# A scan in three stages, spread over the half phases of an eight-part hybrid kernel

## Time and profile before

| | |
|---|---|
| median of the runs | 1622.7 us |
| the profiled execution | 1631.55 us |
| its span, first to last instruction | 1629.8 us |
| mean granted TensorE clock, share of full speed | 0.755 |
| PE, DVE, ACT, POOL busy | 1043.3, 912.9, 745.1, 629.3 us |
| instructions | 18052 |

### The profile page before, as it was taken

The page is one execution under the profiler, slowest core; times in us unless marked ns, Lnnn a source line. Parts: engine busy times, 40 slices in busy tenths (PEclk is TensorE's granted clock), DMA queues, the critical chain, the costliest instruction groups (busy, mean ns, idle before and its releaser), DMA issues.

```text
span 1629.8 us, 18052 instructions
## 1 busy us (share of the span) xinstructions
PE 1043.3 (64%) x5080; PEld 769.7 (47%) x5080; DVE 912.9 (56%) x2789; ACT 745.1 (46%) x2034; POOL 629.3 (39%) x672
## 2 busy tenths in 40 slices
PE   4777788377877554885877624467667536673282
PEld 2454577246664234573755212456456215461172
DVE  4676565485758754656566728164565644646011
ACT  4786676366557544454655413244353232441020
POOL 2102100552414365404232564734443565355503
PEclk8656699587877567787888656788888757886596
DMA  8001243402220122243422211233433222331362
GB/s 246 1 1 66 68 150 110 126 20 104 91 78 12 52 70 78 84 143 100 135 98 65 64 39 43 91 135 102 142 136 110 72 61 87 127 104 47 126 224 90
DMA packets 101812, 150.65 MB, mean 92 GB/s; under 512 B 9840, under 2 KB 72688, under 8 KB 101584
## 3 DMA queue, kind: packets, MB, share of 16 engines
q1 hardware_dynamic: 88832, 129.20, 24.2%
q0 software_dynamic: 8528, 18.19, 3.7%
q10 hardware_dynamic: 4352, 2.10, 0.4%
HBM read 125.39 MB, written 28.25 MB: 94 GB/s over the span
## 4 chain that ended last, share of the span: by engine, by line
PE 33%; DVE 27%; ACT 12%; issue 12%; POOL 9%; DMA 5%; another core or an unknown queue 2%; SPq 1%; POOLq 0%; DVEq 0%; ACTq 0%
DVE Pw L882 9%; PE eo_bank L1290 9%; PE h_bank L1275 8%; ACT sc_bank L635 6%; DVE rings L892 5%; PE sc_bank L1224 5%; POOL xg L562 3%; POOL gbuf L575 2%; DVE nmx L829 2%; PE sc_bank L1168 2%; PE mix_bank L1147 2%; DMA gbuf<-yg,pos 2%; DVE eos L1014 2%; DVE qk L816 2%
## 5 line engine op out<-in xcount | busy, mean ns | idle before, releaser
L1290 PE MATMUL eo_bank<-wring,hid 128*128 128x128 f32 x1472 | 230.5, 307 | 96.9 <-DVE eos L1014 89.3
L882 DVE SCALAR_TENSOR_TENSOR Pw<-rings,bc,du 128x128 f32<-128x128 f32 x512 | 252.3, 553 | 64.8 <-ACT rings L680 64.8
L1275 PE MATMUL h_bank<-xT,wring 128*128 128x128 f32 x1472 | 238.4, 313 | 60.3 <-DVE xT L1002 49.7
L1290 PEld LDWEIGHTS eo_bank<-wring,hid 128*128 128x128 f32 x1472 | 210.9, 220 | 109.4 <-issue 85.2
L1275 PEld LDWEIGHTS h_bank<-xT,wring 128*128 128x128 f32 x1472 | 214.3, 221 | 97.6 <-DVE xT L1002 63.7
L635 ACT ACTIVATE sc_bank<-sc_bank,nmx 128x256 f32<-128x256 f32 x512 | 229.7, 456 | 53.0 <-DVE nmx L829 45.9
L508 POOL TENSOR_TENSOR rings<-Rs,Abc 128x512 f32<-128x512 f32 x128 | 161.9, 1280 | 208.6 <-ACT Rs L663 114.7
L709 ACT ACTIVATE hid<-h_bank 128x512 f32<-128x512 f32 x184 | 109.4, 595 | 286.3 <-PE h_bank L1275 256.2
L1224 PE MATMUL sc_bank<-Pw,upto 128*128 128x512 f32 x256 | 171.2, 769 | 81.0 <-DVE Pw L882 81.0
L829 DVE TENSOR_REDUCE nmx<-sc_bank 128x2 f32<-128x512 f32 x256 | 170.2, 685 | 71.8 <-PE sc_bank L1168 48.8
L575 POOL DMA_INDIRECT gbuf<-yg,pos x128 | 122.6, 957 | 177.9 <-issue 104.1
(11 more groups left out here) (155 smaller groups left out, 1359.2 us busy)
## 6 DMA issues: line engine op xcount, KB each, us to landing
wring<-wcat SPq DMA_DIRECT2D x184, 512.0 KB
stage<-xg SPq DMA_DIRECT2D x40, 256.0 KB
yg<-eos SPq DMA_DIRECT2D x40, 256.0 KB
wcat<-in_w SPq DMA_DIRECT2D x16, 256.0 KB, 5.6
X<-in_x SPq DMA_DIRECT2D x16, 128.0 KB, 5.5
xg<-xnb,pos POOLq DMA_INDIRECT x128
gbuf<-yg,pos POOLq DMA_INDIRECT x128
out<-X ACTq DMA_DIRECT2D x16, 128.0 KB
```

Of the source, the lines that this page charges most:

```text
L882: last = dve.scalar_tensor_tensor(out=Pw[:, c, n * D:(n + 1) * D], in0=e, scalar=bc[:, c, n:n + 1], in1=du[:, c, :], op0=ALU.mult, op1=ALU ...
L1275: last = pe.matmul(hb[b % 2][:, f], wring[:, n % WR, 0, f], xT[:, b % 2], start=True, stop=True)
L1290: last = pe.matmul(eo[:, o:o + P], hid[:, b % 2, f], wring[:, n % WR, 1, f], start=(k == 0), stop=(k == FC - 1))
```

## The change

The scan gets a third stage. A sequence has its front in phase 9 + b, its chunks (`middle`) a phase later and its tail two phases later, so three sequences are in the scan at once; attention goes on in each of phases 0 to 15. There are 33 phases instead of 37. Chunk k's E, L and r stand at half 2k, P at 2k + 1, S at 2k + 2 and X at 2k + 3 of the middle phase (S and X of chunk 7 in the tail's first halves); POOL's phase is now a loop over halves, with exponents at even halves, the first two at halves 13 and 15 of the front's phase.

The chunk sums have one bank of their own, and scores two instead of three. bc, du, Rs, y, uD and xnb are doubled, rec slots are 8. Attention's v moves from the mix bank to the prep bank; the scan's output and the second layer's preparation move from the prep bank to the mix bank, with statistics tiles of their own. A group's 16 scatters go one at each half of a phase, the gathers of the next phase's front one at each of halves 10 to 13, the final gathers at halves 5 to 8. Routing of the second layer moves to the phase after the group's last tail.

Per phase the new schedule has: blocks 9, 10, 4 in phases 6 to 8; 10, 10, 3 in 10 to 12; 10, 10, 3 in 14 to 16; 15, 13, 14, 4 in 17 to 20; 12, 11 in 21 and 22; 13, 10 in 25 and 26; 15, 8 in 29 and 30. Scatters are in phases 5, 9, 13, 16, 17, 20, 24 and 28.

```diff
-    NSC = 3
+    NSC = 2
...
-    FILL = 2 * GS
+    SCAN_FIRST = 2 * GS + 1
...
-        bc = sb("bc", [P, T, 2 * N])
+        bc_b = sb("bc_b", [P, 2, T, 2 * N])
...
         delta = sb("delta", [P, T, P])
-        du = sb("du", [P, T, P])
-        Rs = sb("Rs", [P, T, P])
-
-
-        SLOTS, REC_SLOTS = 4, 6
+        du_b = sb("du_b", [P, 2, T, P])
+        Rs_b = sb("Rs_b", [P, 2, T, P])
+
+
+        SLOTS, REC_SLOTS = 4, 8
         rings = sb("rings", [P, SLOTS + REC_SLOTS, 4 * D])
         Pw = sb("Pw", [P, T, N * D])
         ysum = sb("ysum", [P, 4 * D])
-        y_s = sb("y_s", [P, T, P])
...
-            xnb[ly] = sb(f"xnb{ly}", [P, GT, P])
+            xnb[ly] = sb(f"xnb{ly}", [P, 2, GT, P])
...
+        ss = bank("sum_bank")
...
+        prep_bank = {1: mp, 2: ma}
...
-        AT_LATE = 3
+        GATHER_HALVES = range(10, 14)
+        FINAL_HALVES = range(5, 9)
...
+        scan_dve = Parts(Progress(sem("scan_dve"), ["st0", "stats0", "stats1", "u0", "u", "dpre", "dneg", "delta", "du"]),
+                         Progress(sem("scan_in_dve"), [f"P{k}" for k in chunks]),
+                         Progress(sem("scan_out_dve"), [f"X{k}" for k in chunks]),
+                         Progress(sem("scan_add_dve"), ["x3"]))
...
-        RUN_FIRST = {(1, 0): (6, 1, 40), (1, 1): (10, 1, 60), (1, 2): (17, 1, 46), (2, 0): (20, 1, 46), (1, 3): (25, 1, 30),
-                     (2, 1): (27, 1, 30), (2, 2): (30, 1, 30), (2, 3): (34, 0, 25)}
...
+        RUN_FIRST = {(1, 0): (6, 0, 40), (1, 1): (10, 0, 38), (1, 2): (14, 0, 38), (2, 0): (17, 0, 26), (1, 3): (18, 10, 28),
+                     (2, 1): (21, 0, 32), (2, 2): (25, 0, 30), (2, 3): (29, 0, 25)}
...
-            head[b if b < FILL else FILL + 2 * (b - FILL)] = b
-            tail_a[b + 1 if b < FILL else FILL + 1 + 2 * (b - FILL)] = b
-            f = FILL + 1 + 2 * b if b < FILL else 3 * FILL + (b - FILL)
-            front[f] = b
-            tail_s[f + 1] = b
-        for g, n in enumerate(([23, 24, 25, 26], [29, 30, 31, 31], [32, 33, 33, 33], [36, 36, 36, 36])):
-            for q in range(GS):
-                final.setdefault(n[q], []).append(GS * g + q)
-        PHASES = 37
+            head[b], tail_a[b + 1] = b, b
+            n = SCAN_FIRST + b
+            front[n], middle[n + 1], tail_s[n + 2] = b, b, b
+        final = {n: list(range(b, e)) for n, b, e in ((20, 0, 1), (21, 1, 2), (22, 2, 3), (23, 3, 4), (24, 4, 5), (25, 5, 6), (26, 6, 7), (27, 7, 8),
+                                                      (28, 8, 10), (29, 10, 12), (31, 12, 14), (32, 14, 16))}
+        PHASES = 33
...
-            return [(ly, b // GS) for ly, at in ((1, tail_a), (2, tail_s)) for b in [at.get(n - 1)] if b is not None and b % GS == GS - 1]
...
+            return [(1, tail_a[n - 1] // GS)] if tail_a.get(n - 1, 0) % GS == GS - 1 else \
+                [(2, tail_s[n - 2] // GS)] if tail_s.get(n - 2, 0) % GS == GS - 1 else []
...
+            def scatter_rows(ly, g, n):
 
                 r = RUNS.index((ly, g))
-                pool.wait_ge(*route_dve[ly].at("pos", g))
-                if r:
-                    for j in range(STORES):
-                        pool.wait_ge(s_xg[j], 16 * r)
-                else:
-                    pool.wait_ge(s_zero, 16)
-                for n in range(NSLOT):
-                    pool.indirect_dma_start(xg, bass.IndirectOffsetOnAxis(ap=pos[ly][:, g % 2, n:n + 1], axis=0),
...
+                for half in range(HALVES):
+                    if half == 0 and a is not None:
+                        attn_residual(a)
+                    if half == 0 and ct is not None:
+                        scan_sum(ct, 6)
+                    if half == 2 and ct is not None:
+                        scan_sum(ct, 7)
+                    if half == 3 and ct is not None:
+                        scan_skip(ct)
+                    if half == 3 and c is not None:
+                        scan_rest(c)
+                    if cm is not None and half in range(2, 14, 2):
+                        scan_exponents(cm, half // 2 + 1)
+                    if c is not None and half in (13, 15):
+                        scan_exponents(c, (half - 13) // 2)
+                    if cm is not None and half in (6, 8, 10, 14):
+                        scan_sum(cm, half // 2 - 2)
+                    if cn is not None and half in GATHER_HALVES:
+                        gather_rows(1, cn, half - GATHER_HALVES[0])
+                    if half in FINAL_HALVES:
+                        for b in final.get(n, []):
+                            gather_rows(2, b, half - FINAL_HALVES[0])
+                    for ly, g in scatter_of(n):
+                        scatter_rows(ly, g, half)
...
-                wait_latest(act, (scan_dve, f"X{CHUNKS - 1}", b - 1))
-                act.activation(bc[:], ma[:, L:L + T * 2 * N].rearrange("p (c n) -> p c n", c=T),
...
+                wait_latest(act, (scan_pool, f"arg{CHUNKS - 1}", b - 2))
...
-                if k >= REC_SLOTS:
-                    last = k - REC_SLOTS
-                    act.wait_ge(*scan_pool.at(f"add{last + (last % 4 == 0)}", b))
-                elif k == 0:
-                    wait_latest(act, (scan_pool, "y1", b - 1))
+                wait_latest(act, (scan_pool, f"add{k + (k % 4 == 0)}", b - 1))
...
-                    if half <= 1 and ct is not None:
-                        scan_exps(ct, 7 + half)
...
-                    if 9 <= half < HALVES and c is not None:
-                        scan_exps(c, half - 9)
+                    if half == 13 and tail_s.get(n - 1, 0) % GS == GS - 1:
+                        route_exp(2, tail_s[n - 1] // GS)
...
-                if q == 0 and g:
-                    dve.wait_ge(s_scat, 16 * NSLOT * (RUNS.index((ly, g - 1)) + 1))
...
+                if q == 0 and g >= 2:
+                    dve.wait_ge(s_scat, 16 * NSLOT * (RUNS.index((ly, g - 2)) + 1))
...
-                    if half == 1 and c is not None:
+                    if half == 0 and c is not None:
                         combine(1, c)
                         scan_stats(c)
+                    if half == 1 and ct is not None:
+                        scan_weigh(ct, 7)
                     if half == 2 and c is not None:
                         scan_norm(c)
-                    if half < 4 and ct is not None:
...
-                    if 12 <= half < HALVES and c is not None:
-                        scan_weigh(c, half - 12)
-                    if 9 <= half < HALVES and c is not None:
-                        scan_inputs(c, half - 9)
...
+                    if half % 2 == 1 and half < HALVES and cm is not None:
+                        scan_inputs(cm, half // 2)
+                    if half % 2 == 1 and 3 <= half < HALVES and cm is not None:
+                        scan_weigh(cm, half // 2 - 1)
...
+                    if tail_s.get(n - 1, 0) % GS == GS - 1:
+                        if half == 12:
+                            route_hot(2, tail_s[n - 1] // GS)
+                        if half == 14:
+                            route_weights(2, tail_s[n - 1] // GS)
+                            route_slots(2, tail_s[n - 1] // GS)
+                        if half == 15:
+                            route_rows(2, tail_s[n - 1] // GS)
...
-                    if half == 14:
+                    if half == 13:
...
-                if n - 1 in front:
+                if n - 1 in tail_s:
+                    pe.wait_ge(*prep_dve[2].at("topi", tail_s[n - 1]))
+                elif n - 1 in front:
                     pe.wait_ge(*scan_act.at("R", front[n - 1]))
...
-                    if n in tail_s:
-                        pe.wait_ge(*scan_dve.at(f"X{last_chunk[r]}", tail_s[n]))
-                    elif b:
+                    if b:
                         pe.wait_ge(*attn_act.at(f"exp{last_round[r]}", b - 1))
                 rows = slice(32 * j, 32 * j + 3 * DH)
...
-            def scan_sums(n, b, k):
+            def scan_sums(b, k):
 
                 c, s, _ = quarter(k)
                 pe.wait_ge(*scan_dve.at(f"P{k}", b))
-                if k >= NSC:
-                    pe.wait_ge(*scan_dve.at(f"X{k - NSC}", b))
-                else:
-                    if n - 1 in head:
-                        pe.wait_ge(*attn_act.at(f"exp{last_round[k]}", head[n - 1]))
-                    else:
-                        pe.wait_ge(*scan_dve.at(f"X{last_chunk[k]}", b - 1))
+                wait_latest(pe, (scan_dve, f"X{(k - 1) % CHUNKS}", b if k else b - 1))
                 products = [(upto, Pw[:, c, s])]
                 if c == 1:
                     products += [(ones, Pw[:, 0, s])]
                 for m, (w, v) in enumerate(products):
-                    last = pe.matmul(sc[k % NSC][:], w[:], v, start=(m == 0), stop=(m == len(products) - 1))
+                    last = pe.matmul(ss[:], w[:], v, start=(m == 0), stop=(m == len(products) - 1))
                 last.then_inc(*scan_pe.done(f"S{k}"))
...
```

(31 more changed lines are left out.)

303 lines of the change are left out of this document (147 added, 156 removed).

## The result

The kernel after takes 1675.0 us (median of four runs, 1672.0 to 1678.8) against 1622.9 beside it: 1.034 times as long, interval 1.027 to 1.042. The forecast was 1481 and its range ended at 1580. The rival "lockstep through two banks: slower" said 1663.

A forecast was written before the change was run, and what follows sets the result against it. No engine was taken as near full; in-order engines waiting for each other bound the kernel. Terms 293 + 24 + 489 + 459 + 8 + 214 gave 1487 us of span, scaled to a forecast of 1481, range 1380 to 1580.

The forecast's parts named there:

- lockstep through two banks: slower: Merged phases 10 to 15: scores wait for exps of the same half, 97 us per phase, 1663 in all; chance 11%.
- Two banks for scores: Attention phases 0 to 8: one score bank fewer costs 3.5 us a phase, 31 in all, bounds 2 and 8.
- the burst: POOL's 16 scatters issued together ahead of the scan's exponents, 20.2 us; spreading them takes 7 us off phases 0 to 8.
- I take 77% ... 69 us: Merged attention and scan: three engines near 50 us at a 77% share give 69 us for phases 10, 11, 14 and 15.
- PE's sum k behind X of k - 1 ... inside the 5 us of two halves: Chunk sums on PE: the wait for the previous chunk's X, 0.8 + 1.1 us, fits inside two halves.
- The loss of P to POOL: DVE's P, excluded by POOL's SBUF work, loses 77 us: 252.3 us against 175 at its median.
- the rival that counts on 164: Each of 128 groups of P waits for a whole POOL instruction: 164 us instead of 77, 1568 in all; chance 10%.
- phases with scan and blocks only: Spread chunks in phases 17 to 24: PE decides where blocks stand, 54 to 65 us each; phase 23, without blocks, 45.
- POOL's busy time: Whole span: the same 256 indirect transfers are issued, so POOL stays near 629 us busy.
- the waits for scatters and for the gathers of the fronts: DVE waits of 10 us or more for scatters vanish; combine's wait for its gather falls to near nothing.
- the end: Phase 25 to the final gathers and stores: 214 us, as the same stretch takes today with a whole front in it.
- run starts: Expert runs begin one half after the last scatter: 2 us for each of four runs, 8 in all, upper end 10 each.

The follow-up runs named there:

- The lent bank: The kernel after, with the chunk-sum bank lent to the scores of sequences 0 to 9 as a third bank: 1600.0 us, ratio 0.999 to the kernel before.
- Both orders together: The kernel after, with chunk sums behind scores and blocks on PE and attention's exps ahead of the chunk's functions on ACT: 1576.9 us, ratio 0.970.
- bank edits alone: The kernel after with only the sum bank lent to scores of sequences 0 to 9 (1600.0 us), or only one three-bank pool for scores and sums (1577.2 us).
- c_pool: The kernel after, with sums behind blocks, exps ahead of the chunk's functions, and one pool of three banks for scores and sums: 1499.5 us, ratio 0.922.

## Why the prediction was wrong

**Two banks for scores** is a term of the sum that was mis-sized. I took 3.5 us a phase in phases 0 to 8, within bounds of 2 and 8, and subtracted 7 for the burst. The lent bank shows 61 us / 9 = 6.8. I priced the loop of score, maximum and exp with nothing in it. It costs 5 us a phase without blocks (97 against 81 us for three); in phases 6 and 7 the blocks fall into it too: 22 us for two phases, three times my figure. A second effect I left out: where PE waits more, its granted clock is lower (0.71 in phases 6 and 7 after, 0.83 with the bank lent, 0.93 before), and PE's busy time is longer. With 61 us in place of 31, the mis-sized term accounts for 30 of the 53 us lost in phases 0 to 8. The other 23 stay with the bank lent (309 us against the 286 of the sum without its bank term); 8 of them are in phases 6 and 7 (85 against 77), and the rest was not followed.

**"I take 77% ... 69 us"** is the step that failed. In phases 10 to 15 I forecast 399 us and 494 came. I carried a share of busy time over from stretches in which one or two streams were interleaved, and added a third without following one half through the four queues. The lap at 519 to 529 us shows what the share hides: PE's chunk sum stands ahead of the transposes, ACT's copy waits for these, and the exp stands behind the copy and the functions. Both orders together give 54 of the 95 us; bank edits alone give 0 and 6; orders and pool give 75.

Not only the share was wrong but also the price it was applied to. My prices make 280 us of PE for the six phases (43 blocks at 2.12, six times 13.2 + 18.3), and 353 came. DVE's 310 were 297. The up products of a block and the chunk sums in the stretches that I priced from (1542 to 1602 and 1163 to 1220 us), and then both in phases 10 to 15 of the kernel after:

```profile
L1275 PE MATMUL h_bank<-xT,wring 128*128 128x128 f32 x176 | 25.7, 293 | 4.6 <-DMA wring<-wcat 4.2 <-DVE xT L1002 0.4
```

```profile
L1224 PE MATMUL sc_bank<-Pw,upto 128*128 128x512 f32 x14 | 8.3, 693 | 0.0
```

```profile
L1215 PE MATMUL sum_bank<-Pw,upto 128*128 128x512 f32 x96 | 74.8, 873 | 50.3 <-DVE rings L885 35.7 <-DVE Pw L874 14.5
L1273 PE MATMUL h_bank<-xT,wring 128*128 128x128 f32 x344 | 65.0, 348 | 0.9 <-DVE xT L995 0.9
```

348 ns against 293, 873 against 693, at a granted clock of 0.74 against 0.95 and 0.91. By an estimate from these numbers, 353 / 0.77 = 458, some 59 of the 95 us go with PE's price and 36 with the share, PE's being 0.71. The two may not be independent; no run separates them. In `c_pool` PE is busy 333 of the 419 us, 80%: there the share that I took was reached, and the price is what was short.

**"PE's sum k behind X of k - 1 ... inside the 5 us of two halves"** was wrong too. This wait is 155.9 us in all. In phase 23, without attention and without blocks, the kernel after shows:

```profile
PE sum_bank L1215 <- DVE rings L885: 23.2, 7, 6.1
```

23.2 of 61 us, where I forecast 45. With the pool and both orders the phase takes 49. Of the 21 us that phases 17 to 23 take above the forecast, 16 are in phase 23.

**The loss of P to POOL** I read too low: 252.3 is the busy time of overlapping instructions, while a mean of 553 ns against a median of 342 is 108 us for the 512, not 77. No term of the sum rests on it; the rival that counts on 164 has that much less to add.

**Right** were: phases with scan and blocks only (forecast 401 for 17 to 23, 422 after, 401 with `c_pool`), POOL's busy time (636 us), the waits for scatters and for the gathers of the fronts, the end (280 forecast with the run starts, 282), and that P doesn't meet POOL more often. Most run starts waited for nothing in the kernel after; in `c_pool`, where PE is earlier, they wait 4 to 15 us each.

**The slower rival** named the lap and one of its causes. That its time, 1663, is near the measured one is luck in part: it had 97 us per merged phase and 168 in all from them, and 14 from phases 0 to 8; 82 us, 95 and 53 came. It also laid the lap on the two banks. In the merged phases these cost little as long as PE's order holds the same lap closed; in its text I had the functions ahead of the exp, but not the sum ahead of everything. I gave it 11%, because I argued that P and X run beside the block. In the lap shown it is the sum, the transposes and the exp that don't. The 20 us that `c_pool` still has over my 399 in phases 10 to 15 were not followed further; PE's 333 us against 280 would more than fill them.

## What to carry to other kernels

A share of busy time can't simply be carried to a schedule with one more stream in in-order queues, and neither can a matmul's price from a stretch with a higher granted clock: write out one half with every engine's order, and look for an instruction at a queue's head that waits for another engine's instruction of the same half. Put what waits (a sum into the only free bank, a function that nobody needs yet) behind what others wait for. When buffers are taken from one loop to serve another, price the loop with all that stands in its engines' queues, not with its own instructions; and try a pool before a split: the split cost 6% here (1.034 against 0.971), more than half of it where one of the two users was idle.

## What the hardware showed that I had not expected

The granted clock went down with the waits: the same 19 blocks and two attention sequences ran at 0.93 in 77 us before and at 0.71 in 107 us after, PE's busy time rising from 66.7 to 88.3 us. So a wait for another engine came with slower matmuls on top; which part of the 30 us is the clock's was not separated. In phases 10 to 15 the clock hardly followed the waits: 0.74 in the kernel after, 0.76 in `c_pool`, which waits far less there.

Combine, which reads gathered rows and X from SBUF, took 348 ns each in the kernel before. After (line, busy us, mean ns, idle before):

```profile
L988 DVE SCALAR_TENSOR_TENSOR X<-gbuf,tw,X 128x128 f32<-128x128 f32 x128 | 56.2, 482 | 43.5 <-DMA gbuf<-yg,pos 42.4
```

482 ns. It now runs beside POOL's exponents and sums, while P, spread out, lost less than before (488 against 553). In the trace before, 140 of the 512 P took over 500 ns, and every one of them overlaps a tensor instruction of POOL; a P that meets none took 341 ns in the mean and at most 352, and combine met none. After, 90 P and 18 combines took over 500 ns, again each with one of POOL's beside it. So the exclusion between DVE's two-input work and POOL moved in part from one line to another; what both lost together fell from 109 to 92 us, counted above 342 ns each.
